# k on token partitions: turned from the k already projected instead of projected a second time

## The reference

```
q, k, v = silu(x @ Wq), silu(x @ Wk), silu(x @ Wv)
scores  = (q k^T) * D                      # D: decay to the power of the distance, causal
o       = scores v + (q S) * q_decay       # S: state carried from chunk to chunk
S       = chunk_decay * S + (k * k_decay)^T v
o       = rmsnorm(o * sigmoid(x @ Wg1 @ Wg2)) * w;   y = o @ Wo
```

## Time and profile before

| | us |
|---|---|
| median of 3 runs | 1072.2 (1071.76 to 1073.6) |
| profiled execution, span from first to last instruction, which is taken as its own time | 1074.9 |
| PE busy in the span | 883.8 (82%) |
| DVE busy | 579.7 (54%) |
| ACT busy | 554.3 (52%) |
| POOL busy | 623.6 (58%) |

### The profile page before, as it was taken

How to read it: one execution, slowest core, us unless ns; L and a number is a source line. 1 busy time by engine, 2 the same in 40 slices (tenths; PEclk the granted TensorE clock), 3 DMA queues, 4 the chain that set the end, 5 groups by cost and what they waited for, 6 DMA issues and landing times. The chain is left out here.

```text
span 1074.9 us, 20625 instructions
## 1 busy us (share of the span) xinstructions
PE 883.8 (82%) x5504; PEld 669.3 (62%) x5504; DVE 579.7 (54%) x2104; ACT 554.3 (52%) x1116; POOL 623.6 (58%) x600
## 2 busy tenths in 40 slices
PE   5999899884689899999368998988766999999950
PEld 3566567553578799998233443534326798999840
DVE  4566686866463222326776488674544522222773
ACT  6333456651245455655268776675532555565530
POOL 2465537777677777774730010374664777777773
PEclk9999999986699899999679998988986999999985
DMA  9700002262679876765541011135336798777974
GB/s 337 257 1 1 1 31 87 74 239 96 206 234 298 275 248 213 226 208 170 175 137 35 35 35 35 50 109 210 120 123 184 254 313 270 234 225 239 370 250 153
DMA packets 93231, 181.64 MB, mean 169 GB/s; under 512 B 18985, under 2 KB 73788, under 8 KB 92736
## 3 DMA queue, kind: packets, MB, share of 16 engines
q1 hardware_dynamic: 68544, 114.19, 33.3%
q0 software_dynamic: 24576, 66.13, 16.7%
HBM read 96.34 MB, written 92.27 MB: 175 GB/s over the span
## 5 line engine op out<-in xcount | busy, mean ns | idle before, releaser
L1323 POOL DMA_INDIRECT result_rows<-ys,result_slots x288 | 288.0, 1000 | 98.5 <-issue 83.1
L1007 POOL DMA_INDIRECT expert_rows<-route_rows,index x224 | 222.9, 995 | 67.3 <-issue 64.9
L1981 ACT ACTIVATE b_probs<-ps 128x1024 f32<-128x1024 f32 x128 | 127.7, 1032 | 41.4 <-PE ps L1830 40.7
L1478 PE MATMUL ps<-w_gu,f_xts 128*128 x576 | 109.4, 334 | 1.2 <-issue 1.1
L1478 PE MATMUL ps<-w_gu,g_xts 128*128 x576 | 107.4, 330 | 1.2 <-issue 1.1
L1478 PEld LDWEIGHTS ps<-w_gu,f_xts 128*128 128x128 f32 x576 | 94.2, 194 | 3.4 <-issue 2.8
L1478 PEld LDWEIGHTS ps<-w_gu,g_xts 128*128 128x128 f32 x576 | 93.0, 192 | 2.6 <-issue 2.6
L1575 DVE SCALAR_TENSOR_TENSOR f_h<-ps,f_xs,f_gate 128x96 f32<-128x96 f32 x144 | 39.2, 313 | 89.5 <-ACT f_gate L1530 81.2
L1842 PE MATMUL ps<-b_probs,b_v_pad 128*32 128x512 f32 x512 | 76.8, 675 | 10.1 <-issue 5.1
L1541 ACT COPY ys<-ps 128x512 f32<-128x512 f32 x144 | 83.6, 580 | 1.8 <-PE ps L1497 1.8
L1575 DVE SCALAR_TENSOR_TENSOR g_h<-ps,g_xs,g_gate 128x96 f32<-128x96 f32 x144 | 39.1, 313 | 78.0 <-ACT g_gate L1530 76.6
(11 more groups left out here) (362 smaller groups left out, 1829.4 us busy)
## 6 DMA issues: line engine op xcount, KB each, us to landing
parts<-result_rows SPq DMA_DIRECT2D x32, 896.0 KB, 6.7
f_xs<-expert_rows SPq DMA_DIRECT2D x144, 160.0 KB
g_xs<-expert_rows SPq DMA_DIRECT2D x144, 160.0 KB
expert_rows<-pad_rows SPq DMA_DIRECT2D x64, 160.0 KB
w_gu<-in_Wgu SPq DMA_DIRECT2D x1, 6144.0 KB, 19.4
expert_rows<-pad_rows SPq DMA_DIRECT2D x1, 5120.0 KB, 31.0
result_rows<-ys,result_slots POOLq DMA_INDIRECT x288, 3.5
f_w_d<-in_Wdown SPq DMA_DIRECT2D x1, 4096.0 KB, 15.3
```

What stands on the lines that cost most here:

```text
L1007: self.nc.gpsimd.indirect_dma_start(xs, bass.IndirectOffsetOnAxis(self.index[:, f, t, r:r + 1].bitcast(U32), 0), self.x_rows(f)[:, t, :], ...
L1323: self.nc.gpsimd.indirect_dma_start(self.y_dram, bass.IndirectOffsetOnAxis(self.slots[:, i, j:j + 1].bitcast(U32), 0), self.ys[:, i, j, :] ...
L1478: ins = nc.tensor.matmul(ps[:, bank_gu[u % 2], j * GU:(j + 1) * GU], xts[:, u % 2, o:o + P], w_gu[:, k, bass.ds(experts[j] * GU, GU)], sta ...
L1981: nc.scalar.activation(probs[:, u % RING, :, :], ps[:, 2 * (u % 2):2 * (u % 2) + 2, :], ACT.Exp, scale=float(HD) ** -0.5).then_inc(exp_don ...
```

## The change

Steps 5 and 7 project v alone (256 columns instead of 512). Ahead of that product PE turns the two 128 x 128 blocks of k_t for this tile into the other half of the same bank, for tiles 0 to 2 of a batch; tile 3 is used by no outer product. DVE multiplies the turned k by k_decay straight out of PSUM into k_dec, which now has a place for each tile (`keep_k`); k_tok and its SiLU go. `keep_k` for step 5 runs in units 6 and 14 behind `finish`, for step 7 in unit 0 of the next batch behind `finish`, and for the first half ahead of the split of Wo. The gate product (step 6) and the next step 1 wait for it. `decayed` makes only q_dec, and not for n = 0.

```diff
-        k_tok = sb("k_tok", [P, TT, D])
-        k_dec = sb("k_dec", [P, 2, D])
+        k_dec = sb("k_dec", [P, TT, D])
...
+        def turned_until(g, t):
+            return (TT - 1) * (g // 2) + HT2 * (g % 2) + t
...
                 if s == 1:
                     if some(g):
                         pe.wait_ge(kv_sb, HT2 * g)
+                        pe.wait_ge(k_dec_ready, turned_until(g, 0))
...
-                    product(nc, front, [xt[:, k, t * P:(t + 1) * P] for k in range(KD)],
-                            [w_qkv[:, k, D:3 * D] for k in range(KD)], True, True).then_inc(kv_ready, 1)
+                    if alone and t == 0:
+                        pe.wait_ge(k_sb, 1)
+                    if HT2 * (g % 2) + t < TT - 1:
+                        at = (HT2 * (g % 2) + t) * P
+                        for k in range(KD):
+                            nc.tensor.transpose(front[:, D + k * P:D + (k + 1) * P], k_t[:, k, at:at + P], ident[:, :])
+                    product(nc, front[:, 0:D], [xt[:, k, t * P:(t + 1) * P] for k in range(KD)],
+                            [w_qkv[:, k, 2 * D:3 * D] for k in range(KD)], True, True).then_inc(kv_ready, 1)
                 if s == 6:
                     pe.wait_ge(g1_sb, g + 1)
                     if alone:
                         pe.wait_ge(k_sb, 1)
                     else:
                         pe.wait_ge(kv_sb, HT2 * g + 1)
+                        pe.wait_ge(k_dec_ready, turned_until(g, 1))
...
             def outer_product(n, b):
-                pe.wait_ge(dec_ready, 2 * (TT * b + n) + 1)
+                pe.wait_ge(k_dec_ready, (TT - 1) * b + n + 1)
...
-                    nc.scalar.activation(k_tok[:, HT2 * h + t, :], front[:, 0:D], ACT.Silu)
...
-                nc.vector.tensor_tensor(k_dec[:, n % 2, :].rearrange("p (h e) -> p h e", e=HD),
-                                        k_tok[:, n, :].rearrange("p (h e) -> p h e", e=HD),
-                                        k_decay[:, :, None].broadcast_to([P, H, HD]),
-                                        ALU.mult).then_inc(dec_ready, 1)
...
+            def keep_k(g, t, front):
+                b, tile = g // 2, HT2 * (g % 2) + t
+                if tile < TT - 1:
+                    dve.wait_ge(kv_sb, HT2 * g + t + 1)
+                    if b > 0:
+                        dve.wait_ge(outer_ready, (TT - 1) * (b - 1) + tile + 1)
+                    nc.vector.tensor_tensor(k_dec[:, tile, :].rearrange("p (h e) -> p h e", e=HD),
+                                            front[:, D:2 * D].rearrange("p (h e) -> p h e", e=HD),
+                                            k_decay[:, :, None].broadcast_to([P, H, HD]),
+                                            ALU.mult).then_inc(k_dec_ready, 1)
...
             def body(b):
                 for u in range(UNITS):
                     n, q = u // QUADS, u % QUADS
-                    if q == 0:
+                    if q == 0 and n >= 1:
                         decayed(n, b)
                     weigh(u, b)
...
                     finish(n, q, b)
+                    if u == 0 and not first(b):
+                        keep_k(2 * b, 1, front_of(7, 2 * b))
+                    if is_next(u, b) and u % STEPS_AHEAD == 6:
+                        keep_k(next_half(u, b)[0], 0, front_of(5, next_half(u, b)[0]))
                     if is_next(u, b):
                         g, h = next_half(u, b)
                         project(u % STEPS_AHEAD, g, h, b + (1 if h == 0 else 0))
...
             dve.wait_ge(decay_done, 1)
+            for t in range(HT2):
+                keep_k(0, t, front_of(5 + 2 * t, 0))
             split_rest(dve, late, len(early))
```

More of the change, by code:

```diff
@@ L227, in lightning @@
         q_ready, q_sb, k_ready, k_sb = sem("q_ready"), sem("q_sb"), sem("k_ready"), sem("k_sb")
-        kv_ready, kv_sb = sem("kv_ready"), sem("kv_sb")
+        kv_ready, kv_sb, k_dec_ready = sem("kv_ready"), sem("kv_sb"), sem("k_dec_ready")
         g1_ready, g1_sb = sem("g1_ready"), sem("g1_sb")
@@ L410, in outer_product @@
                     ins = nc.tensor.matmul(ps[:, bank_kv, m * HH * PAD:(m + 1) * HH * PAD],
-                                           k_dec[:, n % 2, m * P:(m + 1) * P],
+                                           k_dec[:, n, m * P:(m + 1) * P],
                                            v_pad[:, n, m * HH:(m + 1) * HH, :], start=True, stop=True)
@@ L426, in output @@
                     if n >= 1:
-                        pe.wait_ge(dec_ready, 2 * (c + 1))
+                        pe.wait_ge(dec_ready, (TT - 1) * b + n)
                 out = ps[:, bank_o, q * P:(q + 1) * P]
@@ L521, in project @@
                     act.wait_ge(kv_ready, HT2 * g + t + 1)
-                    nc.scalar.activation(k_tok[:, HT2 * h + t, :], front[:, 0:D], ACT.Silu)
                     nc.scalar.activation(v_pad[:, HT2 * h + t, :, 0:HD],
-                                         front[:, D:2 * D].rearrange("p (h e) -> p h e", e=HD),
+                                         front[:, 0:D].rearrange("p (h e) -> p h e", e=HD),
                                          ACT.Silu).then_inc(kv_sb, 1)
@@ L667, in decayed @@
                 c = TT * b + n
-                dve.wait_ge(kv_sb, c + 1)
                 dve.wait_ge(q_sb, 2 * b + n // HT2 + 1)
```

## The result

The changed kernel takes 1087.33 us (median of four runs, 1080.02 to 1090.34) beside 1071.98 for the kernel before on the same chip: the ratio is 1.0145, 95% interval 1.0099 to 1.0191. In a second series it was 1086.66 us, ratio 1.0154 (1.0123 to 1.0185). The change costs about 15 us.

The account below looks back on a forecast made before the run. TensorE (PE), busy 51.88 of 57 us, was taken to bound the first stage; stalls 7.5, start -2.3, clock +3.3 and -1.0 sum to +7.5, on 1072.2 giving 1079.7 us, range 1066 to 1087.

Parts of the forecast that it names:

- The new wait: Ahead of the gate product, PE stalls until DVE reads the turned k: seven times, 14.3 us in all.
- PE's saved work: Steps 5 and 7: 0.49 us less PE in 12 tiles, 0.68 in four, 8.6 us; stalled halves keep mostly 0.49.
- the start: First outer product no longer waits for DVE's weight split; scores 2 at about 26.2, not 28.53: 2.3 us won.
- ACT's slack: Four later halves: ACT's 1 to 1.5 us before its sigmoid absorbs part of the stall, leaving 1.1 + 0.7 + 0.6 + 1.2.
- The clock: Behind idle stalls PE restarts at 1.2 GHz: two new episodes, 3.3 us, less 1.0 for an old one near 138 us.
- Rival 1: Faster: stalls fall into PE's idle time before the masks, in scores two units later; -8.0, 1064.2 us; chance 0.17.
- Rival 2: No change: halves with ACT's masks hide the stall entirely and the clock holds; +1.6, 1073.8 us; chance 0.13.
- Rival 3: Slower still: every stall ahead of the gate product also drops the clock; +16.8, 1089.0 us; chance 0.10.
- The forecast's own range: Stalls ahead of the gate product on the path, with none to five clock episodes: 1074.9 to 1085 us; chance 0.60.
- Transposes: 24 turns replacing product columns may not count as PE-busy: one more slow clock episode likely, 1.65 us, 1081.4.
- One for one: At the first stage's end, the barrier before 271.75 us passes every shift on, so stage losses or gains count fully.

Follow-up runs that it names:

- run 4: Kernel before, with DVE multiplying the first tile's k by the decay before splitting the late weights; nothing else differs: 1070.72 us, ratio 0.9995.
- Runs 9: Changed kernel with the eviction of the turned k moved right behind the weighting of units 6 and 14: 1069.96 us, ratio 1.0006.
- 11: Changed kernel with the eviction of the turned k ahead of the weighting in units 6 and 14, measured again: 1066.46 us, ratio 0.9953.
- runs 3: Kernel before with the wait alone: one more DVE operation in units 6 and 14, which the gate product awaits; no k turned: 1088.36 us, ratio 1.0169.
- 14: Kernel before with the wait alone (an extra DVE operation that the gate product awaits), measured again, unedited: 1086.20 us, ratio 1.0142.
- The filled kernel: Changed kernel with three unread products of v on PE ahead of the wait for turned k, in seven halves: 1081.22 us, ratio 1.0092; again 1081.37.
- runs 5: Changed kernel with its 24 turns of k as ordinary f32 products against the identity: 1085.33 us, ratio 1.0120.
- 6: Changed kernel with the eviction ahead of the weighting, and its 24 turns as ordinary products against the identity: 1067.57 us, ratio 0.9956.
- kernel 10: Changed kernel with the eviction ahead of the weighting, plus unread products of v on PE ahead of four mask waits: 1061.38 us, ratio 0.9918.

## Why the prediction was right in direction and wrong in size

**The new wait: right.** Seven pieces were foretold as 1.21, 1.81, 2.34, 2.17, 2.37, 1.74 and 2.69, 14.3 us; they came as 1.22, 1.83, 2.35, 2.19, 2.35, 1.75 and 2.79, 14.5 us. The eviction takes 0.41 us, as bounded by the earlier trace rows.

**PE's saved work and the start: about right in sum.** The forecast kept 0.49 us in six halves and 0.34 in one (3.3 us) and 2.3 us at the start, 5.6 together; the account gives 6.2, as what is left over. A pair of turns holds PE for 0.14 us, not 0.19. Scores 2 came at 25.89 for a forecast of 26.2, and the outer products wait for nothing. But DVE's order is not the whole reason at the start: run 4 makes the first k product ahead of the split as well and gains nothing.

**ACT's slack: failed, 3.5 us.** For the four later halves the prediction let ACT's slack before its sigmoid, the SiLU that it loses and DVE's dropped products take up part of the stall: 1.1 + 0.7 + 0.6 + 1.2 = 3.6 us, where the stalls less PE's saving are 2.17 + 2.37 + 1.74 + 2.69 - 1.81 = 7.2. Runs 9 and 11 show that these halves pay even a wait of 0.63 us whole, which a slack of 1 to 1.5 us would have hidden; runs 3 and 14 show that all seven pay, but for about 1 us. The filled kernel says it from the other side: with its 1.3 us longer hold taken off and its clock set to the kernel before's (0.34 x 6.8 = 2.3 us), its stage end is 7.44 - 1.3 + 2.3 = +8.4, where the prediction's terms without the clock's came to 7.5 - 2.3 = +5.2.

**The clock: failed, some 2.5 to 4.7 us.** The term had two new episodes at 1.65 us and one old one less, +2.3 us. Measured, the clock is at half for 20.4 us more in the typical profile, 7.0 us by the account (4.8 us at the 0.23 of the changed kernel's own two profiles); filling the waits gives back 5.3 and 6.1 us in the medians, with PE held 1.3 us longer. The bound from above (all seven stalls, 11.6 us) did hold it; the choice inside the bounds was too low. The price was not too low: the episode of the earlier trace rows has the clock at half for 3.4 us and was put at 1.65 us, 0.49 for each us, against 0.34 in the account. Too few episodes were counted: in the first profile, five of the seven stalls are followed by one; in the second, three.

With 0.2 for the stalls and -0.6 for the savings, 3.5 + 4.7 makes the 7.8 us that the forecast lacked. This closes because the account was set by the same profile; at the lower price of the clock it is 0.2 + 1.6 + 3.5 + 2.5, with 4.0 us of savings. That both terms were too favourable is shown; how the loss splits between clock and savings is known only within these bounds.

**The rivals.** Rival 1 decides where the masks' waits shrink by over 3.4 us; they shrank by 1.2 in one profile and grew by 0.9 in the other. Rival 2 needed ACT's masks to hide the stall, and no run shows them hiding any. Rival 3, all stalls with a fall of the clock, was sized at 1089.0: its mechanism is the nearest, and a chance of 0.10 was too little, as was the upper end of the range. The forecast's own range, 1074.9 to 1085, has a lower end that its terms do not give: with no episode they come to 7.5 - 2.3 - 1.0 = +4.2, 1076.4 us.

**Transposes.** Turns made as ordinary products leave the times of both kernels about as they were, and 18 turns hold the clock in the filled wait about as 18 passes do (13.6 us at half; 10.3 and 13.6 with products). The Trainium skill (TensorE: Matmul & The Clock Gate, Part 4: PE-mode transpose), which the prediction weighed, says that transposes do not count as PE-busy the same way. No run here shows that in this kernel, and runs 5 and 6 leave room for 2 to 3 us.

**One for one.** What the stage loses reached the end: +15.31 at the stage's end, +15.35 in the medians. That the two agree so closely is chance, but the runs bear the claim out: with stage ends from 262.33 to 287.06 us, what lies behind them took 797.1 to 801.2 us in all the profiles but that of the kernel before (803.2).

## What to carry to other kernels

When an engine's result is moved into a buffer that another engine must empty, look at where that reader stands in its own queue, not at the operation's 0.41 us: here the same change is 15 us slower than the kernel before with the read last of five or six operations of its unit and 4 us faster with it first. An idle wait on TensorE can be charged twice, once for itself and once for the slower clock behind it, so bound the second charge from above when the waits are many. Idle time that cannot be removed may be worth filling with work that nothing reads: here 5.3 and 6.1 us.

## What the runs showed of the hardware

In the same kernel, behind the same wait of 2.35 us at the same place, the granted clock fell to half in one execution and not in another. The row of the first profile is above (gate at 96.03, scores at 97.13 lasting 1.91 us); the changed kernel's second profile has this in its timeline:

```profile
96.11 1.10 PE L398 MATMUL ps<-a_w_g,a_g 128*128 128x256 f32 x4 [2.35 <-DVE a_k_dec L691]
...
97.05 1.02 PE L412 MATMUL ps<-a_q_mask,a_k_t 128*128 128x512 f32 x2
```

Such chance probably moves the runs of one kernel: 1080 to 1093 us for the changed kernel, but only 1059 to 1064 in kernel 10, where the waits for k are gone and four waits for masks are filled. The Trainium skill (TensorE: Matmul & The Clock Gate, Part 1: The HAM clock gate) says of the slow products at a kernel's start that their number varies from run to run of one kernel. The two profiles, 37.5 and 20.5 us at half, show the like in the middle of one. What decides it in an execution stays open, and so does why the wait alone had 20.5 us at half in both of its profiles.
